# A chunk's flag moved to behind the third gather of the next chunk, and the last chunk handled in two halves

## What is computed

```
h = _layernorm(x, axis=-1) * (1 + cb) + sb
gate = softmax(h @ w_gate.T)                    # 8 experts
topk_scores, topk_idx = top_k(gate, 2)          # two experts for each token
y = gelu(h @ W1[e] + b1[e]) @ W2[e] + b2[e]     # 128 -> 512 -> 128, for its two experts
out = x + gb * (score0 * y0 + score1 * y1)      # gb: one vector for each sequence
```

## Time and profile before

| | us |
|---|---|
| three runs: median (lowest to highest) | 810.93 (807.05 to 812.1) |
| the profiled execution | 804.24 |
| its span, first to last instruction | 802.3 |
| POOL busy, of the span | 290.7 (36%) |
| DVE busy, of the span | 440.9 (55%) |
| TensorE busy, of the span | 417.3 (52%) |
| last gather of chunk 15 issued, from the span's start | 790.65 |
| last operation of DVE ended | 799.44 |

### The profile page before, as it was taken

How to read it: one execution, slowest core, us unless ns; L and a number is a source line. 1 busy time by engine, 2 the same in 40 slices (tenths; PEclk the granted TensorE clock), 3 DMA queues, 4 the chain that set the end, 5 groups by cost and what they waited for, 6 DMA issues and landing times.

```text
span 802.3 us, 14898 instructions
## 1 busy us (share of the span) xinstructions
PE 417.3 (52%) x4184; PEld 348.2 (43%) x4185; DVE 440.9 (55%) x1035; ACT 333.3 (42%) x746; POOL 290.7 (36%) x344
## 2 busy tenths in 40 slices
PE   5444773400076500546299999211599935887000
PEld 4334662400065400435099998000498814675000
DVE  7888888301188501655078888010499914666713
ACT  3444884210187210443066765000366603456621
POOL 3281000777300575028600003777000172431773
PEclk9766886655588655668589999555699966798555
DMA  9940334211235211303134334221133322331622
GB/s 236 308 133 1 104 123 126 77 51 52 85 114 156 60 51 40 106 27 93 59 73 93 98 92 111 66 56 52 43 93 97 94 76 56 88 90 51 186 69 65
DMA packets 129680, 73.19 MB, mean 91 GB/s; under 512 B 53744, under 2 KB 122992, under 8 KB 129392
## 3 DMA queue, kind: packets, MB, share of 16 engines
q1 hardware_dynamic: 121456, 56.02, 25.5%
q0 software_dynamic: 8192, 16.79, 7.2%
HBM read 21.75 MB, written 34.90 MB: 71 GB/s over the span
## 4 chain that ended last, share of the span: by engine, by line
PE 40%; issue 28%; DVE 15%; another core or an unknown queue 5%; ACT 5%; POOL 4%; DVEq 1%; DMA 1%; ACTq 1%; SPq 0%; POOLq 0%
PE psA L1160 17%; PE psA L1148 8%; POOL ROW L493 4%; PE psV L1148 4%; PE psH L1148 4%; DVE ATT L753 2%; PE psH L1057 2%; DVE stats L692 2%; PE psA L1066 1%; DVE w_bound L928 1%; PE psA L1068 1%; DVE X L825 1%; PE psA L1067 1%; ACT ATT L589 1%
## 5 line engine op out<-in xcount | busy, mean ns | idle before, releaser
L493 POOL DMA_INDIRECT ROW<-slot_out,POS x128 | 131.6, 1028 | 259.7 <-DMA slot_out<-VP 166.7
L482 POOL DMA_INDIRECT slot_rows<-ROW,POS x128 | 127.7, 998 | 194.1 <-DVE EXPT L903 156.0
L1160 PE MATMUL psA<-WST,ATT 128*128 x2040 | 155.9, 227 | 68.7 <-issue 66.6
L1160 PEld LDWEIGHTS psA<-WST,ATT 128*128 128x128 f16 x2040 | 132.2, 101 | 90.1 <-issue 82.9
L967 DVE TENSOR_SCALAR ATT<-ATT,f_scales 128x1024 f16<-128x1024 f32 x85 | 63.9, 752 | 166.4 <-remote 133.1
L637 ACT ACTIVATE ATT<-psA,b1T,f_scales 128x256 f32<-128x256 f32 x172 | 83.0, 562 | 141.2 <-issue 63.8
L969 DVE SCALAR_TENSOR_TENSOR ATT<-ATT,f_scales 128x1024 f16<-128x1024 f32 x85 | 109.1, 1284 | 3.0
L1148 PE MATMUL psA<-WT,WST 128*128 128x256 f16 x516 | 72.0, 287 | 12.6 <-issue 7.8
L637 ACT ACTIVATE ATT<-psV,b1T,f_scales 128x256 f32<-128x256 f32 x84 | 42.8, 560 | 75.1 <-PE psH L1148 49.2
L1057 PE MATMUL psH<-ident,ATT 128*128 128x128 f32 x64 | 15.1, 379 | 94.2 <-DVE ATT L753 76.5
L1148 PEld LDWEIGHTS psA<-WT,WST 128*128 x516 | 49.8, 102 | 24.8 <-issue 17.4
(11 more groups left out here) (197 smaller groups left out, 723.7 us busy)
## 6 DMA issues: line engine op xcount, KB each, us to landing
slot_out<-VP SPq DMA_DIRECT2D x85, 128.0 KB
slot_rows<-zero SPq DMA_DIRECT2D x9, 1024.0 KB, 5.4
X<-in_x SPq DMA_DIRECT2D x8, 512.0 KB, 7.0
WST<-in_W SPq DMA_DIRECT2D x2, 2048.0 KB, 14.9
WST<-WT SPq DMA_DIRECT2D x16, 256.0 KB
out<-X SPq DMA_DIRECT2D x16, 256.0 KB
slot_rows<-ROW,POS POOLq DMA_INDIRECT x128
GA<-gate_rows SPq DMA_DIRECT2D x1, 2048.0 KB, 9.6
```

The lines of the kernel that those rows point to most:

```text
L482: nc.gpsimd.indirect_dma_start(xg[g], bass.IndirectOffsetOnAxis(ap=POS[:, k * TILES + t:k * TILES + t + 1], axis=0), ROW[:, t * 2 * D:(t + ...
L493: nc.gpsimd.indirect_dma_start(YG[:, o:o + D], None, yg[g], bass.IndirectOffsetOnAxis(ap=POS[:, i:i + 1], axis=0)).then_inc(gathered[c % 2 ...
L1160: last = mm(psD[k % 2][:, h * D:(h + 1) * D], a[:, k % 2, i:i + TOK], W2S[:, ds(e * 2 * FF + b * FF + m * D, D)], start=(m == 0 and c == 0 ...
```

## The change

It is on three engines.

POOL: the flag of chunk c-1 is written behind the third gather of chunk c and not behind the eighth. The eight gathers of chunk 15 are issued in another order: tiles 0 and 1 of both experts first, then tiles 2 and 3, and each four add to a semaphore of their own, `half_in[0]` and `half_in[1]`. There is no flag for chunk 15 any more.

DVE: chunk 15 is mixed in two halves of 2 tiles, each of four operations of half the size; each half waits for its `half_in` directly.

SP: the loop stores chunks 0 to 14; the two halves of chunk 15 are stored by two transfers of 128 KB.

```diff
-            with sp.Fori(0, CHUNKS) as c:
+            with sp.Fori(0, CHUNKS - 1) as c:
                 sp.wait_ge(mixed, c + 1)
                 sp.dma_start(outv[c], X[:, ds(c * CH * D, CH * D)].rearrange("p (t d) -> p t d", d=D)).then_inc(out_done, 16)
-            sp.wait_ge(out_done, 16 * CHUNKS)
+            for h in range(2):
+                sp.wait_ge(mixed, CHUNKS + h)
+                first = (CHUNKS - 1) * CH + h * CH // 2
+                sp.dma_start(outv[CHUNKS - 1][:, h * CH // 2:(h + 1) * CH // 2, :],
+                             X[:, first * D:(first + CH // 2) * D].rearrange("p (t d) -> p t d", d=D)).then_inc(out_done, 16)
+            sp.wait_ge(out_done, 16 * (CHUNKS + 1))
...
-                for k in range(2):
-                    for t in range(CH):
-                        o, i = ((c % YRING) * 2 * CH + k * CH + t) * D, k * TILES + c * CH + t
-                        nc.gpsimd.indirect_dma_start(
-                            YG[:, o:o + D], None, yg[g],
-                            bass.IndirectOffsetOnAxis(ap=POS[:, i:i + 1], axis=0)).then_inc(gathered[c % 2], 16)
+                for n in range(2 * CH):
+                    if c == CHUNKS - 1:
+                        k, t = n // 2 % 2, n // 4 * 2 + n % 2
+                        done = half_in[n // 4]
+                    else:
+                        k, t = n // CH, n % CH
+                        done = gathered[c % 2]
+                    o, i = ((c % YRING) * 2 * CH + k * CH + t) * D, k * TILES + c * CH + t
+                    nc.gpsimd.indirect_dma_start(
+                        YG[:, o:o + D], None, yg[g],
+                        bass.IndirectOffsetOnAxis(ap=POS[:, i:i + 1], axis=0)).then_inc(done, 16)
+                    if n == 2 and c:
+                        landed(c - 1)
...
                 for c in range(G0[g] // CH, (G0[g] + GT[g]) // CH):
                     gather(c, g)
-                    if c:
-                        landed(c - 1)
-            landed(CHUNKS - 1)
...
-            for part in range(4):
-                mix(CHUNKS - 1, CHUNKS - 1 - YRING, part, 3 * MIXED + 2 * (CHUNKS - 1 - MIXED))
+            def mix_half(h, base):
+                c, t = CHUNKS - 1, CH // 2
+                first = c * CH + h * t
+                y = YG[:, (c - YRING) * 2 * CH * D:(c - YRING + 1) * 2 * CH * D].rearrange(
+                    "p (k h t d) -> p k h t d", k=2, h=2, t=t)[:, :, h]
+                dve.wait_ge(half_in[h], 16 * CH)
+                cw = CW[:, :, first:first + t].rearrange("p k (t o) -> p k t o", o=1).broadcast_to([128, 2, t, D])
+                nc.vector.tensor_tensor(y, y, cw, ALU.mult).then_inc(mix_link, 1)
...
+                nc.vector.tensor_tensor(x, x, y[:, 0], ALU.add).then_inc(mixed, 1)
+            for h in range(2):
+                mix_half(h, 3 * MIXED + 2 * (CHUNKS - 1 - MIXED) + 3 * h)
```

More of the change, by code:

```diff
@@ L212, in build_adaln_block @@
         gathered, scaled = [sem(f"gathered{n}") for n in range(2)], sem("scaled")
+        half_in = [sem(f"half_in{h}") for h in range(2)]
         rows_in, mix_link, mixed, out_done = sem("rows_in"), sem("mix_link"), sem("mixed"), sem("out_done")
@@ L1010, in _ @@
                         mix(c, c - first // YRING * YRING, part, 3 * MIXED + 2 * (c - MIXED) - 1, True)
-            for part in range(4):
-                mix(CHUNKS - 1, CHUNKS - 1 - YRING, part, 3 * MIXED + 2 * (CHUNKS - 1 - MIXED))
+            def mix_half(h, base):
[6 more added lines that the diff above has]
+                nc.vector.tensor_tensor(y, y, cw, ALU.mult).then_inc(mix_link, 1)
+                dve.wait_ge(mix_link, base + 1)
+                nc.vector.tensor_tensor(y[:, 0], y[:, 0], y[:, 1], ALU.add).then_inc(mix_link, 1)
+                dve.wait_ge(mix_link, base + 2)
+                gb = GA[:, (2 * c + h) * D:(2 * c + h + 1) * D].rearrange("p (o d) -> p o d", o=1).broadcast_to([128, t, D])
+                nc.vector.tensor_tensor(y[:, 0], y[:, 0], gb, ALU.mult).then_inc(mix_link, 1)
+                dve.wait_ge(mix_link, base + 3)
+                x = X[:, first * D:(first + t) * D].rearrange("p (t d) -> p t d", d=D)
+                nc.vector.tensor_tensor(x, x, y[:, 0], ALU.add).then_inc(mixed, 1)
+            for h in range(2):
+                mix_half(h, 3 * MIXED + 2 * (CHUNKS - 1 - MIXED) + 3 * h)
         @block.tensor
```

## The result

| | before | after |
|---|---|---|
| median of 20 runs, us | 810.88 (807.05 to 816.64) | 806.88 (802.67 to 813.85) |
| ratio to before | | 0.9948, 95% interval 0.993 to 0.9967 |
| profiled execution: time, span | 804.24, 802.3 | 809.41, 807.5 |
| start of chunk 12's first gather | 744.52 | 754.61 |
| from there to the end of the last gather ("the gathers") | 46.13 | 46.67 |

The change makes the kernel 0.5% faster: by the ratio 4.2 us of 811, with an interval of 2.7 to 5.7 us; the two medians differ by 4.0 us. With 20 runs of each kernel 0.5% can be told from none, which three runs could not. The profiled execution of after reached chunk 12 ten us later than that of before. Runs of one kernel differ by as much (807.05 to 816.64 for before), and I take this for such a difference, since the rows show nothing ahead of the mixing that waited for what the change moves.

What follows compares the result with a forecast made beforehand. Bound: the gathers of chunks 12 to 15 (46.1 us), then an 11.65 us tail. New tail 0.84 + 1.64 + 2.1 + 2.86 = 7.45, 4.2 less: 810.93 - 4.2 = 806.7 us, range 801.5 to 811.0.

Steps and rivals of the forecast that it cites:

- The tail waits for chunk 14: After the last gather: the wait ending last is for chunk 14, already landed; this tail was 11.65 us before.
- Flags cost POOL nothing, and three gathers cover the landing: On POOL: moved flags of chunks 0 to 13 count 0; three gathers give 3.75 us against a landing of 1.64.
- the second rival: On POOL: the moved flag waits stall the gathers if a landing exceeds 3.75 us, gain gone from 4.8; chance 0.06.
- the gap: On POOL: one idle time of 2.21 us behind chunk 14's first gather, against a plain 0.30, cause not shown.
- Flag 14 at 39.9 us behind chunk 12's first gather (784.4), chunk 14 mixed at 45.4, the first half at 47.5: On POOL and DVE: flag 14 written at 784.4, chunk 14 mixed at 789.9, first half ended at 792.0.
- Gathers held up by 0.84: In chunk 15: DVE's mixing lengthens three gathers by 0.28 us each, 0.84 in all, bounds 0 and 2.1.
- The first rival: On POOL: each gather beside DVE waits out a whole operation, 0.69 us, leaving a gain of 2.3 us; chance 0.12.
- The landing: Before the second half: rows arrive 1.64 us after the last gather ends, at 793.1.
- A half takes 2.1: On DVE: mixing each half of chunk 15, four operations, takes 2.1 us.
- The end: From DVE's end to the span's end: 2.86 us kept, at most 0.44 less for the smaller store.
- a sign: In the profile after: 2.4 to 2.9 us from the second half's end to the span's end.
- the third rival: On POOL: one more gap like that of 2.21 us (808.6 us) or one less (804.8 us); chance 0.08 each.

Runs made afterwards that it cites:

- halves_only: The changed kernel with the flags back behind the eighth gather of the next chunk, chunk 15 still in halves; ratio 1.0005 to the kernel before.
- flags_only: The kernel before with the flags behind the third gather, chunk 15 whole with its flag, four operations and one store; ratio 0.9952 to the kernel before.
- flag_first: The changed kernel with the flags behind the first gather of the next chunk instead of the third; ratio 0.9881 to the kernel before.
- after_again: The changed kernel itself, measured again with nothing altered; ratio 0.9909 to the kernel before.

## Why the prediction was right, point by point

Forecast 806.7 us, measured 806.88; forecast gain 4.2 us, measured 4.2 by the ratio of the times (4.0 by their medians) and 4.9 by the profiles. The mechanism is the one forecast: the tail waited for chunk 14, and after the change for the last landing. That the time agrees to 0.2 us is luck: the terms of the sum were off by up to 0.6 us, and the interval of the times is 3 us wide. Its steps:

- **The tail waits for chunk 14.** Shown by halves_only and flags_only: without the earlier flag the halves give nothing, with it alone 2.5 us are gained.
- **Flags cost POOL nothing, and three gathers cover the landing.** No flag waited in the profile after. Landings measured 1.56 to 2.25 us over all runs; the second rival wanted 4.8. It is out. That the chain would pay in full what a flag waits was my assumption. In flag_first waits of 1.5 us in all made it 0.1 to 0.2 longer, but there the gap and the meetings with DVE gave back the rest, so the price stays open.
- **Flag 14 at 39.9 us behind chunk 12's first gather (784.4), chunk 14 mixed at 45.4, the first half at 47.5.** Measured 39.8, 45.2, 47.2. These are in part luck: 0.34 us of them are the gap, which was longer than before.
- **Gathers held up by 0.84.** In chunk 15 two gathers were held up, by 0.47 and 0.20, so 0.67. Over all 32 the gathers' busy time rose by only 0.2, because the mixing that moved ahead met others; the stretch grew by 0.54, of which 0.34 is the gap (2.55 for 2.21).
- **The first rival** had the mechanism, and the wrong price. (It took the price of a whole operation from the rule that it cites; by that rule, too, only the rest is waited for.) A gather does wait for the operation of DVE that it meets, but only for what is left of it when the gather begins. Dense mixing costs 0.2 to 0.5 us a gather, not 0.69.
- **The landing** before the second half took 1.90 us, and 1.86 in after_again, not 1.64: 0.26 too little. It was 1.64 in before, where no store was issued within 4 us of the gather's end, and in flag_first, whose half's store began 1.3 us before the gather's end; 1.9 where that store began 0.6 us behind it; and 2.24 with the flag in flags_only, where 256 KB were sent from 1.0 us before it. No run changes the store alone, so that the stores lengthen the landing is not shown.
- **A half takes 2.1.** 2.08 and 2.06.
- **The end took 2.24 and 2.30 us**, and I had kept 2.86 and given 0.44 as the most that a smaller store might save. It saved 0.6, and the end fell out of the 2.4 to 2.9 that I had named as a sign. In the eight runs whose last store has 128 KB the end took 2.24 to 2.32 us, in the two with 256 KB 2.86 and 2.91, so it goes with the size of the store. This is the term that was mis-sized most.
- **The gap** of the third rival stayed one gap, at the same gather, 2.55 us for 2.21.

So the sum from chunk 12 on, 53.6, was 0.7 too high: 0.6 from the store, 0.3 from the gathers, against 0.26 for the landing. The errors are under what the times can tell; the profiles show them.

## What to carry to other kernels

Where an engine works through a written order, look in the tail for an event that lies ready but whose announcement stands behind unrelated work, and move it behind just enough of that work to cover its latency; the cover needed is read from one row. Splitting the last piece pays only once nothing else is queued ahead of it: test the parts alone, since they may be in series. And price a shared resource by what is left of the other's operation when the two meet, not by the whole.

## What the runs showed that I had not expected

While POOL issues indirect gathers one behind the other (1.25 us each) beside the loop over the slots, TensorE, DVE and ACT nearly stop, from about ten us after the first until some ten after the last. What TensorE waited for in the kernel before from 504 to 564 us, by the trace:

```profile
PE psA L1160 <- issue: 32.5, 21, 3.9
PE psV L1148 <- issue: 14.0, 6, 2.4
```

It is no semaphore and no transfer that the profile shows; single matmuls stand 1 to 4 us apart. The granted clock is 0.50 there, the lower of its two levels (1.2 GHz), but a matmul takes 0.27 to 0.37 us and the gaps are several times that, so the clock is not what stops it. Nor does the profile show code being loaded: in the kernel before it has no packet of the instruction queues between 490 and 640 us. The same is seen beside scatters ahead of the loop: from 280 to 315 us TensorE runs 4 matmuls and DVE nothing, and DVE goes on at 315.70, as the last scatter of that group ends. Pauses of mostly 0.7 to 1.0 us, in place of 0.30, behind most second gathers remove most of it: 33 matmuls became 577 in the same 60 us. The mixing loops of ACT and DVE at the end of the program run at their usual 2.44 and 0.69 us beside back-to-back gathers, so it does not strike all work alike. What stands behind it is open, and with it whether the pause or the smaller number at a time is what helps.
